# Two chunk transpositions of a five-hop graph kernel, and the powers of its last rows, done another way

## What is computed

```python
h = relu(adj @ (x @ L0_W1) + b1)            # hop 0
h = relu(adj @ (h @ L0_W2) + b2)            # hop 1
x = layernorm(x + h)
f1 = adj @ x @ L1_W1                        # hops 2, 3 and 4
f2 = adj @ adj @ x @ L1_W2
f3 = adj @ adj @ adj @ x @ L1_W3
x = layernorm(x + (f1 + f2 + f3) / 3.0)
```

## Time and profile before

| | before |
|---|---|
| median of 3 runs | 256.37 us (255.79 to 256.46) |
| the profiled execution, its own time | 256.48 us |
| its span in the profile | 254.7 us |
| PE busy, share of the span | 247.2 us, 97% |
| DVE busy | 200.9 us, 79% |
| ACT busy | 193.1 us, 76% |
| POOL busy | 16.7 us, 7% |
| granted PE clock | 0.999 of 2.4 GHz |

### The profile page before, as it was taken

One profiled execution on the slowest core, in us unless ns is written; L12 is line 12 of the kernel. 1 busy time (PEld: TensorE's weight loads), 2 busy tenths in 40 slices (PEclk: granted clock), 3 DMA queues, 4 the chain that ended last, 5 costly groups with the idle time before them and its releaser, 6 DMA issues.

```text
span 254.7 us, 3758 instructions
## 1 busy us (share of the span) xinstructions
PE 247.2 (97%) x1152; PEld 204.3 (80%) x1152; DVE 200.9 (79%) x391; ACT 193.1 (76%) x337; POOL 16.7 (7%) x24
## 2 busy tenths in 40 slices
PE   8999999999999999999999999999999999999991
PEld 8688788888888888877888888888888888888880
DVE  0898899796789889898778777767676767888844
ACT  2897998886868787978877787867677776788751
POOL 1000000000003021130000000000000000303032
PEclk9999999999999999999999999999999999999999
DMA  6999999920000000000000000000000000010111
GB/s 213 389 386 385 387 386 387 400 91 0 0 3 3 0 0 3 0 0 1 0 4 0 0 0 3 0 0 1 4 0 0 0 3 0 0 42 0 45 41 42
DMA packets 11396, 20.49 MB, mean 80 GB/s; under 512 B 1264, under 2 KB 2288, under 8 KB 11248
## 3 DMA queue, kind: packets, MB, share of 16 engines
q1 hardware_dynamic: 11088, 19.93, 21.4%
q10 hardware_dynamic: 288, 0.33, 0.4%
HBM read 19.20 MB, written 1.05 MB: 80 GB/s over the span
## 4 chain that ended last, share of the span: by engine, by line
PE 82%; SPq 5%; DMA 4%; DVE 3%; ACT 2%; issue 2%; POOL 0%; POOLq 0%; DVEq 0%; ACTq 0%
PE filters L393 17%; PE filters L386 17%; PE filters L387 17%; PE pair L393 9%; PE pair L386 9%; PE pair L387 9%; DMA adj<-a_t 4%; SPq L271 3%; PE weighted L361 2%; PE turned L363 2%; ACT ring_high L517 2%; DVE ring_low L632 1%; SPq L269 1%; SPq L275 1%; DVE operand_low L586 1%
## 5 line engine op out<-in xcount | busy, mean ns | idle before, releaser
L632 DVE TENSOR_TENSOR ring_low<-adj,ring_high 128x512 fp32r<-128x512 f32 x240 | 160.0, 688 | 34.8 <-ACT ring_high L517 32.0
L517 ACT ACTIVATE ring_high<-adj 128x512 fp32r<-128x512 f32 x240 | 148.6, 629 | 32.7 <-PE filters L387 15.9
L386 PE MATMUL filters<-ring_high,operand_low 128*128 128x512 f32 x156 | 62.0, 398 | 0.0
L393 PE MATMUL filters<-ring_low,operand_high 128*128 128x512 f32 x156 | 61.2, 392 | 0.4 <-DVE ring_low L632 0.4
L387 PE MATMUL filters<-ring_high,operand_high 128*128 128x512 f32 x156 | 60.8, 390 | 0.0
L393 PEld LDWEIGHTS filters<-ring_low,operand_high 128*128 128x128 f32 x156 | 29.3, 188 | 8.0 <-DVE ring_low L632 1.8
L387 PEld LDWEIGHTS filters<-ring_high,operand_high 128*128 128x128 f32 x156 | 29.3, 188 | 5.7
L386 PEld LDWEIGHTS filters<-ring_high,operand_low 128*128 128x128 f32 x156 | 29.3, 188 | 5.7
L386 PE MATMUL pair<-ring_high,operand_low 128*128 128x512 f32 x84 | 33.3, 396 | 0.0
L393 PE MATMUL pair<-ring_low,operand_high 128*128 128x512 f32 x84 | 33.1, 394 | 0.2
L387 PE MATMUL pair<-ring_high,operand_high 128*128 128x512 f32 x84 | 32.7, 390 | 0.0
(11 more groups left out here) (84 smaller groups left out, 209.0 us busy)
## 6 DMA issues: line engine op xcount, KB each, us to landing
adj<-a_t SPq DMA_DIRECT2D x48, 256.0 KB, 9.6
resident_raw<-a_t SPq DMA_DIRECT2D x16, 256.0 KB, 9.7
nodes<-x_rows SPq DMA_DIRECT2D x1, 1024.0 KB, 11.6
lead<-lead_in SPq DMA_DIRECT2D x3, 256.0 KB, 4.7
out_rows<-nodes SPq DMA_DIRECT2D x3, 256.0 KB, 2.4
lead<-lead_in ACTq DMA_DIRECT2D x1, 192.0 KB, 2.9
lead<-lead_in SPq DMA_DIRECT2D x1, 128.0 KB, 2.7
lift_raw<-lifts SPq DMA_DIRECT2D x1, 128.0 KB, 11.3
```

The source lines that it names most:

```text
L386: nc.tensor.matmul(bank, y_low, a_high, start=first, stop=False)
L393: used = nc.tensor.matmul(bank, y_high, a_low, start=False, stop=last)
L517: nc.scalar.activation(ring_high[:, n % RING, :], source, ACT.Copy).then_inc(high_ready, 1)
L632: nc.vector.tensor_tensor(ring_low[:, n % RING, :], source, ring_high[:, n % RING, :].bitcast(F32), ALU.subtract).then_inc(low_ready, 1)
```

## The change

It has two parts.

**Chunks 0 and 1 of hop 2.** Their posts go from PE. Instead DVE transposes `chunk_t` (128 x 512) in blocks of 32 x 32 with one instruction per chunk, right behind the ring item after the evacuation (`turn_blocks`), into `turned_blocks`. SP then moves the 16 blocks of each tile to their places in `turned_rows`: 16 transfers a chunk, each of 32 partitions x 4 tiles x 32 numbers, which is 16 KB in 128 runs of 128 bytes. ACT and DVE make the operands from `turned_rows` once all 16 have landed. The two buffers lie where the operands of hop 3 will be, so no memory is added. The operand work moves back: from 4 steps after the chunk's end to 19 (chunk 0), and from 8 to 25 (chunk 1). The post of chunk 2, which stays on PE, moves from 4 to 10.

**The end.** Three pieces become two halves. POOL takes the powers column by column, four instructions instead of three. DVE applies the norm to all four tiles, ACT to none. There are two stores of 128 KB: SP issues the first, ACT the second. PE puts the residual of tile 3 into its bank after the first two sums, not before them.

```diff
+BLOCK = 32
+BLOCK_TRANSFERS = 16 * (P // BLOCK) ** 2
+BY_BLOCKS = {(2, 0): 19, (2, 1): 25}
+POSTS_AFTER = {(2, 2): 10, **BY_BLOCKS}
...
-    return end_of(hop, c) + (8 if (hop, c) == (2, 1) else 4)
+    return end_of(hop, c) + POSTS_AFTER.get((hop, c), 4)
...
-PIECES = (slice(0, 2), slice(2, 3), slice(3, 4))
...
+        turned_blocks = nc.alloc_sbuf_tensor_at("turned_blocks", [P, 2, TILES, D], F32, offset=place[0])
         operand_high = sb("operand_high", [P, 2, TILES, D], F32R)
+
+        turned_rows = nc.alloc_sbuf_tensor_at("turned_rows", [P, 2, TILES, D], F32, offset=place[0])
         operand_low = sb("operand_low", [P, 2, TILES, D], F32R)
...
+        def visited(hop, c):
+
+            return hop * CHUNKS + c + 1 - sum(chunk <= (hop, c) for chunk in BY_BLOCKS)
+
+        def by_blocks(hop, c):
+
+            return sum(chunk <= (hop, c) for chunk in BY_BLOCKS)
...
+        last_banks = [weighted[:, 0, :], weighted[:, 1, :], turned[:, 0, :], pair[:, 0, 0:D]]
...
+            for n, (hop, c) in enumerate(BY_BLOCKS):
+                tiles = slice(c * TPC, (c + 1) * TPC)
+                sp.wait_ge(blocks_turned, n + 1)
+                for i in range(0, P, BLOCK):
+                    for j in range(0, P, BLOCK):
+                        sp.dma_start(turned_rows[j:j + BLOCK, (hop + 1) % 2, tiles, i:i + BLOCK],
+                                     turned_blocks[i:i + BLOCK, (hop + 1) % 2, tiles, j:j + BLOCK]
+                                     ).then_inc(rows_in[n], 16)
...
-            for piece in range(1, len(PIECES)):
-                tiles = last_tiles(piece)
-                sp.wait_ge(last_normalised, piece)
-                sp.dma_start(out_rows[:, tiles, :], nodes[:, tiles, :]).then_inc(out_stored, 16)
-
-            sp.wait_ge(out_stored, 16 * (CHUNKS - 1 + len(PIECES)))
+            sp.wait_ge(last_normalised, half_tiles)
+            sp.dma_start(out_rows[:, last_tiles(0), :], nodes[:, last_tiles(0), :]).then_inc(out_stored, 16)
+
+            sp.wait_ge(out_stored, 16 * (CHUNKS - 1 + HALVES))
...
-            for piece, part in enumerate(PIECES):
-                pool.wait_ge(variance_ready, whole_groups * HALVES + piece + 1)
-                nc.gpsimd.tensor_tensor(rstd[:, part], variance[:, part], exponent[:, part], ALU.pow
-                                        ).then_inc(rstd_ready, 1)
+            for half, part in enumerate(halves):
+                pool.wait_ge(variance_ready, whole_groups * HALVES + half + 1)
+                for t in range(part.start, part.stop):
+                    nc.gpsimd.tensor_tensor(rstd[:, t:t + 1], variance[:, t:t + 1], exponent[:, t:t + 1], ALU.pow
+                                            ).then_inc(rstd_ready, 1)
...
-                elif hop in (0, 2, 3) and c > 0:
+                elif hop in (0, 3) and c > 0:
                     pe.wait_ge(operand_low_ready, operands(hop, c - 1))
-                elif hop in NORMED and c > 0:
+                elif hop == 1 and c > 0:
                     pe.wait_ge(residual_added, residuals(hop, c - 1))
-                elif hop == 2:
+                elif (hop, c) == (2, 2):
                     pe.wait_ge(residual_added, CHUNKS)
+                elif (hop, c) == (2, 3):
+                    pe.wait_ge(operand_low_ready, operands(hop, c - 1))
+                elif hop == 4 and c > 0:
+                    pe.wait_ge(residual_added, residuals(hop, c - 1))
...
-                        if (h, chunk) != (HOPS - 1, CHUNKS - 1) and post_step(h, chunk) == at:
+                        if (h, chunk) != (HOPS - 1, CHUNKS - 1) and (h, chunk) not in BY_BLOCKS and post_step(h, chunk) == at:
...
-            for piece in range(len(PIECES)):
-                nc.tensor.matmul(piece_bank(piece), ident[:], nodes[:, last_tiles(piece), :], start=True, stop=False)
-            for piece, part in enumerate(PIECES):
-                pe.wait_ge(chunk_evacuated, HOPS * CHUNKS + part.start // half_tiles)
-                for t in range(part.start, part.stop):
-                    last = nc.tensor.matmul(piece_bank(piece)[:, t - part.start, :], chunk_t[:, t * P:(t + 1) * P],
-                                            ident[:], start=False, stop=(t == part.stop - 1))
-                last.then_inc(post_multiplied, 1)
+
+            def add_sums(t):
+                return nc.tensor.matmul(last_banks[t], chunk_t[:, t * P:(t + 1) * P], ident[:], start=False, stop=t > 0)
+
+            first_half = nodes[:, last_tiles(0), :]
+            nc.tensor.matmul(weighted[:, 0:half_tiles, :], ident[:], first_half, start=True, stop=False)
+            nc.tensor.matmul(last_banks[2], ident[:], nodes[:, TILES - 2, :], start=True, stop=False)
+            pe.wait_ge(chunk_evacuated, HOPS * CHUNKS)
+            add_sums(0)
+            add_sums(1).then_inc(post_multiplied, 1)
+            nc.tensor.matmul(last_banks[3], ident[:], nodes[:, TILES - 1, :], start=True, stop=False)
+            pe.wait_ge(chunk_evacuated, HOPS * CHUNKS + 1)
+            add_sums(2)
+            add_sums(3).then_inc(post_multiplied, 1)
...
-                if hop or c:
-                    act.wait_ge(post_multiplied, hop * CHUNKS + c)
+                before = (hop, c - 1) if c else (hop - 1, CHUNKS - 1)
+                if before in BY_BLOCKS:
+                    act.wait_ge(blocks_turned, by_blocks(*before))
+                elif hop or c:
+                    act.wait_ge(post_multiplied, visited(*before))
...
+                elif (hop, c) in BY_BLOCKS:
+                    act.wait_ge(rows_in[by_blocks(hop, c) - 1], BLOCK_TRANSFERS)
+                    source = turned_rows[:, (hop + 1) % 2, part, :]
                 else:
-                    act.wait_ge(post_multiplied, hop * CHUNKS + c + 1)
+                    act.wait_ge(post_multiplied, visited(hop, c))
                     source = turned[:] if hop == 2 else weighted[:]
...
-            act.wait_ge(shift_ready, whole_groups * HALVES + 1)
-            for t in range(half_tiles):
-                nc.scalar.activation(nodes[:, TILES - TPC + t, :], weighted[:, t, :], ACT.Identity, bias=shift[:, t:t + 1],
-                                     scale=rstd[:, t:t + 1]).then_inc(normalised, 1)
-            tiles = last_tiles(0)
-            act.wait_ge(normalised, whole_groups * TPC + half_tiles)
-            act.dma_start(out_rows[:, tiles, :], nodes[:, tiles, :]).then_inc(out_stored, 16)
+            act.wait_ge(last_normalised, TPC)
+            act.dma_start(out_rows[:, last_tiles(1), :], nodes[:, last_tiles(1), :]).then_inc(out_stored, 16)
...
+            def turn_blocks(hop, c):
+                blocks = turned_blocks[:, (hop + 1) % 2, c * TPC:(c + 1) * TPC, :].rearrange("p t d -> p (t d)")
+                dve.wait_ge(chunk_evacuated, hop * CHUNKS + c + 1)
+                nc.vector.transpose(blocks, chunk_t[:]).then_inc(blocks_turned, 1)
...
+                if hop == 2 and (hop, c) in BY_BLOCKS:
+                    source = turned_rows[:, (hop + 1) % 2, part, :]
...
+                for hop, c in evacuations(n - 1):
+                    if (hop, c) in BY_BLOCKS:
+                        turn_blocks(hop, c)
...
-            done = HOPS * CHUNKS - 1
-            for piece, part in enumerate(PIECES):
-                m = whole_groups * HALVES + piece
-                dve.wait_ge(post_multiplied, done + piece + 1)
-                for t in range(part.start, part.stop):
-                    last = nc.vector.bn_stats(stats[:, t, :], piece_bank(piece)[:, t - part.start, :])
-                last.then_inc(stats_ready, 1)
-
-                dve.wait_ge(shift_ready, whole_groups * HALVES)
-                dve.wait_ge(stats_ready, m + 1)
-                for t in range(part.start, part.stop):
-                    last = nc.vector.bn_aggr(moments[:, t, :], stats[:, t, :])
-                last.then_inc(moments_ready, 1)
-                dve.wait_ge(moments_ready, m + 1)
-                nc.vector.tensor_scalar(variance[:, part], moments[:, part, 1], EPS, None, ALU.add
-                                        ).then_inc(variance_ready, 1)
-            norm_shift(HOPS - 1, CHUNKS - 1, 0)
-            for piece in range(1, len(PIECES)):
-                t = PIECES[piece].start
-                dve.wait_ge(rstd_ready, whole_groups * HALVES + piece + 1)
-                nc.vector.tensor_scalar(nodes[:, TILES - TPC + t, :], piece_bank(piece)[:, 0, :], moments[:, t, 0:1],
-                                        rstd[:, t:t + 1], ALU.subtract, ALU.mult).then_inc(last_normalised, 1)
+            hop, c = HOPS - 1, CHUNKS - 1
+            for half in range(HALVES):
+                dve.wait_ge(post_multiplied, visited(HOPS - 1, CHUNKS - 2) + half + 1)
+                norm_stats(hop, c, half, last_banks[halves[half]])
+                norm_moments(hop, c, half)
+            for t in range(TPC):
+                dve.wait_ge(rstd_ready, whole_groups * HALVES + t + 1)
```

(36 more changed lines are left out.)

3 lines of the change are left out of this document (1 added, 2 removed).

## The result

| | before | after |
|---|---|---|
| median of 6 runs | 256.36 us | 259.3 us (257.83 to 259.64) |
| the profiled execution, its own time | 256.48 us | 259.64 us |
| its span | 254.7 us | 257.8 us |
| granted PE clock | 0.999 | 0.992 |

The ratio is 1.011, with a 95% interval from 1.009 to 1.013: slower by 2.9 us, where 0.8 us faster was forecast. Of the six runs, those with a granted clock of 0.990 to 0.992 took 259.2 to 259.6 us, the two with 0.998 took 257.8 and 258.4.

What follows compares the result with a forecast made beforehand. PE was taken to bound the kernel, with no slack. -0.88 for two posts and +0.10 for the end make -0.78, so 255.6 us against 256.37; range 255.0 to 257.8.

Steps and rivals of the forecast that it cites:

- What bounds the kernel: PE, busy all of each stretch from 125.50 to 247.00; later work moves forward by all that PE loses.
- the posts: Hop 2, PE: two posts of 0.44 us go, 0.88 us, and nothing on PE takes their place.
- The transpositions: Hop 2, DVE: two of 128 x 512, taken at 0.69 us each, costing nothing on the path.
- the distance from issue to issue: SP's 32 block transfers: 0.475 us from one issue to the next, so no stall was forecast.
- The other price: Engines moving the data: 33 to 76 ns a packet, so one transfer occupies them for 0.30 to 0.68 us.
- Rival (b): Chunk 1's blocks come late and PE stands still in front of item 144: 258.2 us at 0.68 a transfer; chance 0.21.
- its dates: ACT reaches chunk 0's operand at 136.4 and chunk 1's at 143.3; chunk 1 can land as late as 146.3.
- the last harmless landing: Latest landing of rows before PE stands still: 146.3 for chunk 1, 138.3 for chunk 0.
- the rival's own sum: Chunk 1 lands at 125.6 + 31p + 2.2, p us from one transfer to the next; 148.9 at 0.68.
- Its price: Rival (b): each 0.1 beyond 0.60 a transfer costs 3.1 us of PE standing still; at 0.68, 2.6 us late.
- The end: Behind PE's last step, with residual moved, four powers and a lone last store: +0.1 us, bounds -0.2 and +0.7.

Runs made afterwards that it cites:

- the run with POOL's copies: The changed kernel with 16 copies on POOL replacing the 16 transfers of a chunk, operand dates unchanged; 254.9 us, ratio 0.9952.
- source in HBM: The changed kernel with the 32 transfers reading from input x in HBM, same runs of 128 bytes, output not the reference's; 255.29 us.
- four transfers: The changed kernel with 4 transfers a chunk instead of 16, each 32 partitions x 2 KB in place, output not the reference's; 254.26 us.
- the kernel with three chunks: The changed kernel with chunks 0, 1 and 2 of hop 2 by blocks, POOL moving 0 and 2, SP 1; 254.19 us, ratio 0.9933.
- wide: The changed kernel with each of the 32 transfers copying 128 partitions x 32 numbers, blocks not put in their places; 259.51 us.
- long: The changed kernel with each of the 32 transfers copying 32 partitions x 128 numbers in place, 32 runs of 512 bytes; 258.59 us.

## Why the prediction was wrong

**What bounds the kernel** was read rightly. PE has no slack. The kernels in which PE didn't wait for an operand give the posts back whole: the distance is 0.94, 0.93 and 0.93 shorter for the 0.88 of two posts (POOL, source in HBM, four transfers) and 1.40 for the 1.32 of three. Where SP moved chunk 0 at 0.64 and ACT waited for it, it is less: 0.73 for two, 0.34 for the 0.44 of one.

**The transpositions** were sized rightly: 0.70 us, where 0.69 had been taken from the ring's row.

```profile
124.52 0.70 DVE L579 STREAM_TRANSPOSE turned_blocks<-chunk_t 128x512 f32<-128x512 f32 x1
```

They cost PE nothing: the runs that give the posts back whole have them too.

**The step that failed is the distance from issue to issue.** I took 0.475 us, "these have 128 rows, and the new ones 128 runs". The likeness of shape was no argument: the runs with other shapes show that shape doesn't count, and the run from HBM shows that the source does. All rows from which I took the price had one end in HBM. The other price was wrong to the other side and harmless: share 0.15 of 16.50 us x 16 engines = 39.6 us, over 16.5 / 0.645 x 144 = 3680 packets, is 11 ns a packet, not 33 to 76. The engines that move the data were nearly idle; SP's issuing alone was the bound. In "DMA: Bandwidth & Descriptors" the Trainium skill says, in the section Issuing engines are not separate DMA queues, that the time to start a transfer is usually small beside the transfer. Here it wasn't: 0.60 us of issue stood against 0.1 us of moving (9 packets of 11 ns). The same section says that issuing on several engines saves only that time; here it would have been the time that counts, but no run issued blocks from a second queue. What the runs show is that fewer issues (four transfers a chunk) or another engine for part of the blocks (the kernel with three chunks) take the stall away. The same page's rule on transfers under 64 KB, which the prediction had set against this part, agrees in its direction: 64 KB cost the same 0.60 as 16 KB.

**Rival (b) was what happened, and its dates held within 0.3 us.** They have to be counted from the evacuation of chunk 0, since that came at 122.69 in the profiled execution and at 123.05 before. So counted, ACT was to ask for chunk 1 at 20.25 and asked at 20.50, and the last harmless landing was 23.25. With 0.645 the rival's own sum, 125.6 + 31 x 0.645 + 2.2 = 147.8, is a landing at 24.75; it was 25.06, as a few of the first issues took longer and the landing itself only 1.84. That is 1.8 us late, where the rival's sum makes 1.5 of it, and 257.1. (The likeness of 147.8 and the 147.75 of the trace is partly luck.) I gave (b) 0.21, although 0.59 stood in the same rows and the margin from 0.475 to 0.60 was the thinnest in the sum. Yet even 0.59 would have landed the rows at 146.1, just in time: no row of before had the price that decided.

For chunk 0 the last harmless landing was put too late. It was 138.3, or 137.9 in the time of this execution; the rows landed at 137.45, before it, and PE lost 0.24 us.

**Its price was too small.** Measured is 259.3, above the range. Two terms were missing. The 1.8 us make a first gap as long, and then the ring refills item by item, 2.8 us in all. And PE's clock fell afterwards, 1.6 us more, which no term foresaw. In sum: -0.88 + 0.24 + 2.8 + 1.6 = +3.8, and the distance is 3.80 longer. The spans differ by only 3.1, since the end is 0.34 shorter and the evacuation of chunk 0 came 0.36 earlier, which is scatter of the loads at the start.

That the clock is a cost of its own is borne out by the six executions. A fall of 3.4 us to half, in a span of 258, takes 0.007 off the mean clock. The two executions with 0.998 can't have had it. They took 257.8 and 258.4, the four others 259.2 to 259.6, about 1.4 more. And 256.36 - 0.88 + 0.24 + 2.8 - 0.3 for the end = 258.2. These two were not profiled, so that their gap was the same is likely, not shown. Even they lie at or above the top of the range.

**The end** was to cost 0.1 and gave about 0.3. The chain of waits of the changed kernel:

```profile
252.98 1.06 POOL rstd L344 x2
254.04 0.51 POOLq L135
254.55 0.52 POOL rstd L344
...
255.09 0.41 DVE nodes L700
```

Four powers take 2.1 us, not 2.2, since they overlap a little, and the last one ends 4.67 us after the last matmul's start (250.40), where it was 251.59 - 246.96 = 4.63. So the powers give and take nothing, nearly as worked out; the gain lies behind them, where the lone last store is. As the landing of that store scatters (1.9 us here, 2.6 in the run with POOL's copies) and there is one trace of before, that the store is the cause is likely, not shown.

## What to carry over

Before work goes to an idle engine or queue, price it by a row with the same two ends, not the same shape; if the trace has none, the bound from another kind of transfer is no bound. Write down the date at which the consumer in order reaches the result, and the last harmless date behind it, and compare both with a landing at each end of the price: here the dates were right to 0.3 us and one price decided the sign. A late operand on an engine that works in order costs more than its lateness, since the buffers behind it are empty, and where TensorE is the bound its clock can come on top. A busy share of 100% doesn't say that an engine lost nothing, where its instructions overlap: compare the distances between starts.

## What the runs showed of the hardware

The median issue on SP's queue took 0.60 us with both ends in the core's memory (16 KB in 128 runs, on 32 or 128 partitions) and 0.59 with 32 runs of 512 bytes or with 64 KB. From HBM into the core's memory it took 0.43 for 16 KB, and for 256 KB in hop 0 0.43 at first and 0.55 in the median; from the core's memory to HBM 0.33 to 0.35 for 64 to 256 KB. POOL copies 32 partitions x 128 numbers to other partitions in 0.28 to 0.80 us, one every 0.56 on average, and DVE items beside it took up to 0.78 instead of 0.69 us. VectorE's transposition of 128 x 512 numbers in blocks took 0.70 us.

In three profiled executions with a first gap of 1.65 to 1.83 us (the changed kernel, wide and long) TensorE went on at 1.2 GHz for 3.4 us, from 1.1 us (long) or 2.3 us (the two others) after the gap's end on; in between it worked in pieces. After a gap of 1.15 us with the same kind of pieces it kept 2.4 GHz. The length of the gap may not be all: by their mean clock of 0.998 two unprofiled executions of the changed kernel kept it too, and nothing tells that their gap was shorter.
